# Scan-stage statistics moved from DVE to ACT and POOL, and expert gathers dealt out between the weight splits

## The chip, the cores and the metric

The kernel runs on one core of a Trainium2 chip. The time is the device time of one execution in microseconds (us). Three runs are shown: 2676.52, 2685.60 and 2686.33 us, median 2685.6. The profile is of one further execution. Engines: PE is TensorE (PEld its weight loads), DVE is VectorE, ACT is ScalarE, POOL is GpSimd, SP is SyncE, which issues most of the DMAs.

## The reference, cut to what matters

Two layers on x of shape (4, 512, 512): cross-attention and a gated feed-forward with Hadamard rotations, then a selective scan and a routed mixture of experts. Of it this case needs:

```
# layer norm, ahead of each block
(x - mean) / sqrt(var + 1e-5)
# layer 0 feed-forward: gate and up (512 -> 2048), silu(gate) * up, down (2048 -> 512), added to x
# layer 1 scan: 4 batches x 512 channels x 16 states, along 512 tokens
state = state * exp(delta * A) + (delta * u) * B_t ;  y_t = sum over states of state * C_t
y = (y + D * u) * silu(z)        # z: the layer norm of x; y is added to x
# layer 1 experts: 16 experts 512 -> 256 -> 512, two chosen for each of the 2048 tokens,
# silu(x Wg) * (x Wu) Wd, weighted and summed, beside one shared expert
```

## The kernel before, in words

`build` (L2700) runs stages one after the other, with a barrier of all engines behind each: `stage_norm`, `stage_attention`, `stage_prep`, `stage_mix`, `stage_norm_router`, `stage_experts`, `stage_combine`. Within a stage every engine has its own program, and the order is written out by hand; semaphores tie them together. The residual `xs` stays in SBUF, 16 tiles of 128 tokens x 512 (4 batches of TB = 4).

**The scan stage** (`stage_mix`, L1383) does two things at once: the feed-forward of layer 0 and the scan of layer 1. It has 64 steps s = 16 b + j: batch b, and j both a block of 128 hidden columns of the feed-forward and a scan state. In each step TensorE makes `gate` and `up` for two steps ahead (12 products each) and one `down` (four fp32 products) for three steps back. ACT makes four `decay` (an Exp into a PSUM tile) and one `silu`, and needs two table loads for it. POOL makes four `force` (the drive term, L1786) and three `add` (L1771), over a ring of RING = 4 tiles. DVE makes four `scan` (L1839, then a product L1850, for the first channel tile also a sum L1856), one `inner` (hT, L1864) and one `add_y` (L1870, adds the down product to x). The decays use two PSUM tiles in turn (BANKS = 2), so that decay q waits for the product of scan q - 2:

```
if ft == 0 and fn:
    act.wait_ge(s_add, dve_adds(fp, fn))
else:
    act.wait_ge(s_term, q - BANKS + 1)
```

In steps 0 to 3 of a batch DVE also makes `bn_stats` of one tile of the next batch (`normal_stats`, L1873) and one of the batch before, whose feed-forward is complete by then (`gate_stats`, L1877). At step 4 `spread` (L1879) turns them into `rstd` and `shift`: `bn_aggr`, then `newton_rsqrt` (L104), 14 operations of 4 or 8 columns that each wait for the one before, and the shift. From these, ACT normalizes the next batch (`norm`, L1687, from step 4) for its rotation, and makes `z` (L1713, steps 7 to 10) for the gating of the batch before. POOL has `skip_add` (four a batch at steps 1 to 3) and `gated` (steps 8 to 11). Behind the last step a tail does the last four downs, their statistics, `spread`, `z`, the gating and the transposes, one after the other.

**The expert stage** (`stage_experts`, L2424). The (token, choice) pairs lie sorted by expert in TILES = 47 tiles of 128 rows. For tile k: ACT copies the gathered rows (`fetch`, L2537), TensorE turns them, ACT and DVE split them into a high and a low part (fp32r), TensorE makes the gate and up product (`exp_g`, 12 products), ACT the SiLU, DVE the product, then the down product. The rows come by 47 indirect DMAs which POOL issues (L2507), all of them ahead of its other work, in groups; a group's rows are told to ACT (`s_rows`) when the next group is issued. Weights: SP loads each expert in three pieces into `raw` (two buffers) and `raw_down` (one); the next down piece waits until the one before is split. The split makes w = high + low in a ring of WRING = 3 experts. DVE makes the first three, high and low, ahead of its tiles (L2579, L2581); POOL the other 13 (L2522, L2525), each when the expert three before it is finished:

```
end = pool.value_load(plan.ends[0:1, e - WRING:e - WRING + 1], min_val=0, max_val=TILES)
wait_apart(pool, s_y, end + 2, s_pace)
```

## Time and profile before

| | |
|---|---|
| runs (median; lowest, highest) | 2685.6 us (2676.52; 2686.33) |
| the profiled execution | 2678.03 us |
| its span, first to last instruction | 2676.2 us |
| busy in the span: PE, DVE, ACT, POOL | 2285.0 (85%), 1848.7 (69%), 1229.4 (46%), 1354.8 us (51%) |
| mean granted TensorE clock | 0.926 |
| first and last scan start (L1839) | 1434.8 and 2140.5 us |
| first gather and first product of the experts | 2297.9 and 2328.4 us |
| last expert product starts | 2615.6 us |
| first gather of the combine stage | 2620.96 us |

Busy shares of the whole span mix stages with different limits; the rows below are of single stretches. In a timeline a bracket gives the idle time of the engine ahead of the instruction and what ended it. In a group, "x16 | 10.9, 682" is 16 instructions, 10.9 us in all, 682 ns each on average.

### The profile page before, as it was taken

To read this page: it belongs to the slowest core of one execution; us is meant where nothing else is said; L and a number is where in the kernel's file an instruction comes from. 1 tells how busy PE (TensorE), PEld (TensorE's weight loads), DVE (VectorE), ACT (ScalarE), POOL (GpSimd) and SP (SyncE) were. 2 spreads that over 40 slices of the span, in tenths; PEclk is the share of its full clock that TensorE was granted. 3 is DMA by queue.
4 is the path that set the end of the run, shared out by engine and by line. 5 is a ranking of instruction groups with operands and counts; after the bars stand their busy time and mean duration, and the time that the engine had idled before them with its cause. 6 is when DMAs were issued, how large, how long until landed. Compare 5 with 4: busy or idle time off the path is not lost. (4 is left out here: it accounts for less than half of the span.)

```text
span 2676.2 us, 35075 instructions
## 1 busy us (share of the span) xinstructions
PE 2285.0 (85%) x10784; PEld 1760.5 (66%) x10785; DVE 1848.7 (69%) x3381; ACT 1229.4 (46%) x2129; POOL 1354.8 (51%) x1088
## 2 busy tenths in 40 slices
PE   3799999999999999998774998897998969468980
PEld 2688888878888888887433665665665547347770
DVE  6577776767676777766775999999999976312223
ACT  2344444544454544444573655655655622124430
POOL 0233333333333333333584888878978931678324
PEclk7799999999999999999887999998998988789995
DMA  7512232222323122220557555564665321765317
GB/s 283 221 67 88 87 111 88 85 74 84 111 87 112 68 87 87 87 88 20 185 194 226 173 183 189 172 197 142 208 183 163 122 83 48 248 170 176 121 51 263
DMA packets 136761, 363.49 MB, mean 136 GB/s; under 512 B 21264, under 2 KB 58768, under 8 KB 118416
## 3 DMA queue, kind: packets, MB, share of 16 engines
q1 hardware_dynamic: 123504, 328.30, 35.8%
q0 software_dynamic: 6320, 20.71, 2.5%
q10 hardware_dynamic: 6768, 12.32, 1.2%
q8 instruction: 94, 1.54, 0.2%
q14 instruction: 75, 0.61, 0.1%
HBM read 289.99 MB, written 71.30 MB: 135 GB/s over the span
## 5 line engine op out<-in xcount | busy, mean ns | idle before, releaser
L641 POOL TENSOR_SCALAR att_probs<-att_probs,att_recip 128x512 f32<-128x512 f32 x256 | 182.1, 714 | 560.8 <-DVE att_recip L708 560.8
L1786 POOL TENSOR_TENSOR mix_drive<-mix_du,mix_rows 128x512 f32<-128x512 f32 x256 | 326.7, 1283 | 63.0 <-DMA mix_rows<-bc_d 24.5
L565 ACT ACTIVATE att_probs<-att_s,att_bias,att_rq 128x512 f32<-128x512 f32 x256 | 200.5, 783 | 287.6 <-DVE att_bias L704 287.2
L1839 DVE TENSOR_TENSOR_SCAN mix_state<-mix_state,mix_drive 128x512 f32<-128x512 f32 x256 | 312.7, 1221 | 16.1 <-POOL mix_drive L1786 11.6
L1670 ACT ACTIVATE mix_state<-mix_delta,mix_a 128x512 f32<-128x512 f32 x256 | 176.7, 691 | 278.4 <-DVE mix_drive L1850 238.6
L1771 POOL TENSOR_TENSOR mix_y<-mix_y,mix_drive 128x512 f32<-128x512 f32 x180 | 230.8, 1282 | 78.7 <-DVE mix_drive L1850 78.7
L1579 PE MATMUL mix_down<-mix_wd,mix_hT 128*128 128x512 f32 x512 | 232.7, 597 | 8.6 <-DVE residual_x L1870 8.6
L703 DVE TENSOR_REDUCE att_nmax<-att_s 128x1 f32<-128x512 f32 x256 | 174.9, 683 | 69.3 <-PE att_s L101 62.0
L744 DVE TENSOR_TENSOR att_pT<-att_pt,att_pT 128x512 fp32r<-128x512 f32 x256 | 170.0, 685 | 65.6 <-ACT att_pT L571 61.6
L571 ACT CAST att_pT<-att_pt 128x512 fp32r<-128x512 f32 x256 | 144.2, 593 | 133.0 <-PE att_pt L422 128.7
L99 PE MATMUL att_w<-att_w_qkv,att_cx 128*128 128x256 f32 x512 | 158.4, 309 | 34.5 <-DVE att_w_qkv L690 26.4
L1579 PEld LDWEIGHTS mix_down<-mix_wd,mix_hT 128*128 128x128 f32 x512 | 97.5, 191 | 110.5 <-issue 96.2
L101 PE MATMUL att_w<-att_w_qkv,att_cx 128*128 128x256 f32 x512 | 152.5, 298 | 0.0
L100 PE MATMUL att_w<-att_w_qkv,att_cx 128*128 128x256 f32 x512 | 152.3, 297 | 0.0
L422 PE MATMUL att_pt<-att_ident,att_probs 128*128 128x128 f32 x1024 | 142.1, 277 | 6.6 <-DVE att_pT L744 2.3
L650 POOL TENSOR_TENSOR att_rq<-att_qss,att_power 128x8 f32<-128x8 f32 x32 | 55.6, 1737 | 159.2 <-DVE att_qss L740 159.2
L422 PEld LDWEIGHTS att_pt<-att_ident,att_probs 128*128 128x128 f32 x1024 | 118.8, 144 | 22.1 <-DVE att_pT L744 12.0
L99 PEld LDWEIGHTS att_w<-att_w_qkv,att_cx 128*128 128x128 f32 x512 | 105.0, 205 | 39.8 <-issue 37.3
L1850 DVE TENSOR_TENSOR mix_drive<-mix_state,mix_rows 128x512 f32<-128x512 f32 x180 | 124.4, 691 | 6.2
L99 PE MATMUL exp_g<-exp_w,exp_xT 128*128 x188 | 81.9, 436 | 53.2 <-POOL exp_w L2525 34.8
L579 ACT CAST att_oT<-att_o 128x512 fp32r<-128x512 f32 x64 | 37.7, 589 | 181.0 <-PE att_o L101 181.0
L99 PE MATMUL att_s<-att_kT,att_qT 128*128 128x512 f32 x256 | 106.7, 417 | 14.0 <-issue 9.1
(356 smaller groups left out, 6655.5 us busy)
## 6 DMA issues: line engine op xcount, KB each, us to landing
att_xn<-normT SPq DMA_DIRECT2D x32, 2048.0 KB, 8.7
mix_gu<-guT SPq DMA_DIRECT2D x64, 1024.0 KB, 8.2
mix_rows<-bc_d SPq DMA_DIRECT2D x128, 256.0 KB, 5.1
guT<-att_ffnT SPq DMA_DIRECT2D x32, 512.0 KB, 5.7
mix_wd<-wdT SPq DMA_DIRECT2D x16, 1024.0 KB, 7.8
slots<-exp_y ACTq DMA_DIRECT2D x47, 256.0 KB, 2.0
normT<-nrm_outT SPq DMA_DIRECT2D x4, 2048.0 KB, 9.1
exp_raw<-in_L_ffn_Wg SPq DMA_DIRECT2D x16, 512.0 KB, 5.8
```

Source lines behind the costliest of these rows:

```text
L99: pe.matmul(out, lh, rh, start=start, stop=False)
L101: return pe.matmul(out, ll, rh, start=False, stop=stop)
L422: tr = pe.transpose(ps_pt[(b + n) % 2][:, t, :], probs[:, h * TB + t, k * P:(k + 1) * P], ident_sb[:, :])
L565: act.activation(probs[:, n, :], ps_s[n % 2][:, :], ACT.Exp, bias=bias[:, n:n + 1], scale=rq[:, n:n + 1], accum_out=sums[:, n:n + 1]).then ...
L641: pool.tensor_scalar(probs[:, n, :], probs[:, n, :], recip[:, n:n + 1], 1.0, ALU.mult, ALU.mult).then_inc(s_pn, 1)
L703: own.after(dve.tensor_reduce(nmax[:, n:n + 1], ps_s[n % 2][:, :], AX_X, ALU.max, negate=True))
L744: dve.tensor_tensor(pT[:, 1, k, :], ps_pt[(b + (TB + 1) * h + k) % 2][:, :, :].rearrange("p t n -> p (t n)"), pT[:, 0, k, :].bitcast(F32), ...
L1579: mm = pe.matmul(ps_y[:, :], hT[c % 2][:, k, tok], wd[c % 2][:, k, :], start=(k == 0), stop=(k == CHUNK - 1))
L1670: act.activation(state[q % BANKS][:, :], delta[i % DELTAS][:, :], ACT.Exp, scale=a[:, t, n:n + 1]).then_inc(s_decay, 1)
L1771: pool.tensor_tensor(out[:, :], out[:, :], drive[q % RING][:, :], ALU.add).then_inc(s_padd, 1)
L1786: pool.tensor_tensor(drive[q % RING][:, :], du[i % DUS][:, :], rows[g % ROWS][:, 0, :], ALU.mult).then_inc(s_drive, 1)
L1839: dve.tensor_tensor_scan(h[:, :], h[:, :], drive[q % RING][:, :], 0.0, ALU.mult, ALU.add).then_inc(s_scan, 1)
```

## The change

In the scan stage the statistics leave DVE. ACT makes them in steps 0 to 3 (`stats`), behind the step's last decay: for each tile an Identity whose accumulator gives the sum, a multiply that gives the negative mean, and a Square of x minus the mean whose accumulator gives the sum of squares; the full-size outputs go to `normT` and are not used. POOL makes `rstd` with `pow` and the shift (`spread`), at step 5, behind the first `add` and `force`. In the tail ACT and POOL do the same for the last batch. In the expert stage the gathers come in groups of 2, 6, 10, 16, 4, 4, 4 and 1: POOL issues the second group when expert 0's weights have landed, the third when expert 1's have, and the last four groups behind its splits of experts 3, 4, 5 and 6. ACT makes the high parts of the first three experts, DVE only the low ones, and the third expert's come behind tile 0. What is computed stays the same. The diff, cut:

```diff
+                summed, centred, squared = Steps(act, s_sums), Steps(act, s_minus), Steps(act, s_squares)
+
+                def moments(tiles):
+                    squared.wait()
+                    for c, row in tiles:
+                        summed.mark(act.activation(normT[:, c // TB, :], xs[:, row, :], ACT.Identity,
+                                                   accum_out=sums[:, c:c + 1]))
+                    summed.wait()
+                    for c, row in tiles:
+                        centred.mark(act.mul(minus[:, c:c + 1], sums[:, c:c + 1], -1.0 / DIM))
+                    centred.wait()
+                    for c, row in tiles:
+                        squared.mark(act.activation(normT[:, c // TB, :], xs[:, row, :], ACT.Square, bias=minus[:, c:c + 1],
+                                                    accum_out=squares[:, c:c + 1]))
+
+                def stats(b, t):
+                    tiles = []
+                    if b + 1 < B:
+                        tiles.append((t, (b + 1) * TB + t))
+                    if b:
+                        act.wait_ge(s_yadd, BLOCKS * (b - 1) + (CHUNK - 1) * TB + t + 1)
+                        tiles.append((TB + t, (b - 1) * TB + t))
+                        if t == 0:
+                            act.wait_ge(s_rot, KD * min(b, B - 1))
+                    moments(tiles)
...
@@ -1736,6 +1763,10 @@
                     if s + 1 < ALL:
                         decay(q + 2)
                         decay(q + 3)
+                    if j < TB:
+                        stats(b, j)
+                    if j == TB:
+                        squared.wait()
...
                 for t in range(TB):
+                    stats(B, t)
+                for t in range(TB):
...
+                def spread(b, done):
+                    c = slice(0 if b + 1 < B else TB, 2 * TB if b else TB)
+                    if b and b + 1 < B:
+                        pool.wait_ge(s_nrm, TB * b)
+                    if b >= 2:
+                        pool.wait_ge(s_z, TB * (b - 1))
+                    pool.wait_ge(s_squares, done)
+                    pool.tensor_scalar(var_eps[:, c], squares[:, c], 1.0 / DIM, LN_EPS, ALU.mult, ALU.add).then_inc(s_var, 1)
+                    pool.wait_ge(s_var, b + 1)
+                    pool.tensor_tensor(rstd[:, c], var_eps[:, c], power[:, c], ALU.pow).then_inc(s_root, 1)
+                    pool.wait_ge(s_root, b + 1)
+                    pool.tensor_tensor(shift[:, c], minus[:, c], rstd[:, c], ALU.mult).then_inc(s_rs, 1)
...
                     for q in range(ET * (s + 1), ET * (s + 2)):
                         add(q - RING)
                         if s + 1 < ALL:
                             force(q)
+                        if j == TB + 1 and q % ET == 0:
+                            spread(b, moments_made(b))
...
                     skip_add(B - 1, t)
+                spread(B, moments_made(B))
...
-                def normal_stats(b, t):
-                    own.mark(dve.bn_stats(stats[:, t, :], xs[:, b * TB + t, :]))
-
-                def gate_stats(b, t):
-                    dve.wait_ge(s_yadd, BLOCKS * b + (CHUNK - 1) * TB + t + 1)
-                    own.mark(dve.bn_stats(stats[:, TB + t, :], xs[:, b * TB + t, :]))
-
-                def spread(first, last):
-                    c = slice(first, last)
-                    own.wait()
-                    for t in range(first, last):
-                        own.mark(dve.bn_aggr(meanvar[:, t, :], stats[:, t, :]))
-                    own.wait()
-                    own.after(dve.tensor_scalar(var_eps[:, c], meanvar[:, c, 1], LN_EPS, None, ALU.add))
-                    newton_rsqrt(dve, own, rstd[:, c], var_eps[:, c], guess[:, c], newton[:, c])
-                    dve.scalar_tensor_tensor(shift[:, c], meanvar[:, c, 0], -1.0, rstd[:, c], ALU.mult,
-                                             ALU.mult).then_inc(s_rs, 1)
...
-                    if j < TB:
-                        if b + 1 < B:
-                            normal_stats(b + 1, j)
-                        if b:
-                            gate_stats(b - 1, j)
-                    if j == TB:
-                        if b and b + 1 < B:
-                            dve.wait_ge(s_nrm, TB * b)
-                        if b >= 2:
-                            dve.wait_ge(s_z, TB * (b - 1))
-                        spread(0 if b + 1 < B else TB, 2 * TB if b else TB)
...
                 for n in range(ALL - LAG - 1, ALL):
                     add_y(n)
-                    gate_stats(B - 1, n % TB)
-                dve.wait_ge(s_z, TB * (B - 1))
-                spread(TB, 2 * TB)
...
-    GROUPS = [4, 4] + [8] * 4 + [7]
+    GROUPS = [2, 6, 10, 16, 4, 4, 4, 1]
...
+                def gather(g):
+                    for k in range(sum(GROUPS[:g]), sum(GROUPS[:g + 1])):
                         pool.indirect_dma_start(rows[:, k, :], None, xn,
                                                 bass.IndirectOffsetOnAxis(plan.source[:, k:k + 1], 0)
                                                 ).then_inc(s_gather[g], 16)
-                        k += 1
-                    if g:
-                        pool.wait_ge(s_gather[g - 1], 16 * GROUPS[g - 1])
-                        pool.sem_inc(s_rows, GROUPS[g - 1])
-                pool.wait_ge(s_gather[-1], 16 * GROUPS[-1])
-                pool.sem_inc(s_rows, GROUPS[-1])
-                for e in range(WRING, EXPERTS):
+
+                def gathered(g):
+                    pool.wait_ge(s_gather[g], 16 * GROUPS[g])
+                    pool.sem_inc(s_rows, GROUPS[g])
+
+                def loaded(e):
+                    for _, _, sem, value in pieces(e):
+                        pool.wait_ge(sem, value)
+
...
+                gather(0)
+                loaded(0)
+                gather(1)
+                gathered(0)
+                loaded(1)
+                gather(2)
+                gathered(1)
+                gather(3)
+                gathered(2)
+                for e in range(WRING, EXPERTS):
+                    g = e - WRING + 3
+                    split(e)
+                    if g < len(GROUPS):
+                        gathered(g)
+                    if g + 1 < len(GROUPS):
+                        gather(g + 1)
...
+                def split_hi(e):
+                    for src, cols, sem, value in pieces(e):
+                        act.wait_ge(sem, value)
+                        act.copy(w[:, e, 0, cols], src[:, :]).then_inc(s_split, 1)
-                tiles(act, step)
+                fetch(0, 0)
+                fetch(1, 1)
+                split_hi(0)
+                x_hi(0, 0)
+                split_hi(1)
+                tiles(act, step, lambda: split_hi(2))
...
-                for e in range(WRING):
+                def split_lo(e):
                     for n, (src, cols, sem, value) in enumerate(pieces(e)):
                         dve.wait_ge(sem, value)
-                        dve.tensor_copy(w[:, e, 0, cols], src[:, :]).then_inc(s_split, 1)
                         dve.wait_ge(s_split, 2 * e + n + 1)
                         dve.tensor_tensor(w[:, e, 1, cols], src[:, :], w[:, e, 0, cols].bitcast(F32),
                                           ALU.subtract).then_inc(s_w if n else s_wpart, 1)
...
-                tiles(dve, step)
+                split_lo(0)
+                x_lo(0, 0)
+                split_lo(1)
+                tiles(dve, step, lambda: split_lo(2))
```

## Rows read from the trace of the kernel before

**Rows 1.** Scan stage, second batch: us; PE, PEld, DVE, ACT, POOL busy; clock; DMA share; GB/s.

```profile
1608.00:1790.00 182.00, 166.22 (x580) 108.91 (x580) 166.56 (x215) 105.97 (x129) 154.82 (x123) 0.96 0.56 179
```

**Rows 2.** Groups of instructions, DVE: line, operation, count, busy us, mean ns, idle before.

```profile
L1877 DVE BATCH_NORM_STATS2 mix_stats<-residual_x 128x6 f32<-128x512 f32 x16 | 10.9, 682 | 0.1
```

**Rows 3.** Tile mix_hT (made once a step), windows: count, min/median/max ns, first and last start.

```profile
L1864 DVE SCALAR_TENSOR_TENSOR mix_hT<-mix_up,mix_up_scale,mix_sil x5: 749/750/751, 1449.6 to 1488.7; 128x512 f32<-128x512 f32 x5
...
L1864 DVE SCALAR_TENSOR_TENSOR mix_hT<-mix_up,mix_up_scale,mix_sil x2: 751/751/751, 1488.7 to 1504.4; 128x512 f32<-128x512 f32 x2
...
L1864 DVE SCALAR_TENSOR_TENSOR mix_hT<-mix_up,mix_up_scale,mix_sil x5: 741/749/751, 1618.4 to 1665.7; 128x512 f32<-128x512 f32 x5
...
L1864 DVE SCALAR_TENSOR_TENSOR mix_hT<-mix_up,mix_up_scale,mix_sil x2: 741/746/752, 1665.7 to 1683.8; 128x512 f32<-128x512 f32 x2
...
L1864 DVE SCALAR_TENSOR_TENSOR mix_hT<-mix_up,mix_up_scale,mix_sil x5: 741/743/751, 1982.2 to 2027.2; 128x512 f32<-128x512 f32 x5
...
L1864 DVE SCALAR_TENSOR_TENSOR mix_hT<-mix_up,mix_up_scale,mix_sil x2: 743/746/749, 2027.2 to 2045.2; 128x512 f32<-128x512 f32 x2
```

**Rows 4.** Timeline of a plain step: start us, us, engine, line, operation.

```profile
1501.74 1.23 DVE L1839 TENSOR_TENSOR_SCAN mix_state<-mix_state,mix_drive 128x512 f32<-128x512 f32 x1 [0.29 <-ACT mix_state L1670]
...
1507.68 0.69 ACT L1670 ACTIVATE mix_state<-mix_delta,mix_a 128x512 f32<-128x512 f32 x1 [1.35 <-DVE mix_drive L1850]
...
1511.40 1.23 DVE L1839 TENSOR_TENSOR_SCAN mix_state<-mix_state,mix_drive 128x512 f32<-128x512 f32 x1
```

**Rows 5.** Groups of instructions, ACT.

```profile
L565 ACT ACTIVATE att_probs<-att_s,att_bias,att_rq 128x512 f32<-128x512 f32 x256 | 200.5, 783 | 287.6 <-DVE att_bias L704 287.2
...
L1670 ACT ACT_TABLE_LOAD x64 | 82.1, 1283 | 1.2
...
L565 ACT ACTIVATION_READ_ACCUMULATOR att_probs<-att_s,att_bias,att_rq 128x1 f32 x256 | 50.7, 198 | 0.0
...
L553 ACT ACTIVATE att_qsq<-att_w 128x512 f32<-128x512 f32 x64 | 40.9, 639 | 0.0
...
L1719 ACT ACTIVATE mix_a<-mix_a 128x64 f32<-128x64 f32 x1 | 0.3, 256 | 0.0
```

**Rows 6.** Waits in the scan loop: us in total, times, longest.

```profile
DVE mix_state L1839 <- POOL mix_drive L1786: 11.6, 7, 3.0
```

**Rows 7.** Groups of instructions, POOL.

```profile
L1786 POOL TENSOR_TENSOR mix_drive<-mix_du,mix_rows 128x512 f32<-128x512 f32 x256 | 326.7, 1283 | 63.0 <-DMA mix_rows<-bc_d 24.5 <-DVE mix_state L1839 15.4 <-DMA mix_du<-du_d 8.7
...
L650 POOL TENSOR_TENSOR att_rq<-att_qss,att_power 128x8 f32<-128x8 f32 x32 | 55.6, 1737 | 159.2 <-DVE att_qss L740 159.2
```

**Rows 8.** Timeline of the scan stage's tail: DVE, then ACT.

```profile
2161.04 0.69 DVE L1877 BATCH_NORM_STATS2 mix_stats<-residual_x 128x6 f32<-128x512 f32 x1
...
2165.44 3.16 ACT L1713 ACTIVATE mix_work<-residual_x,mix_shift,mix_rstd 128x512 f32<-128x512 f32 x4 [11.28 <-DVE mix_shift L1887]
```

**Rows 9.** Timeline of POOL in the expert stage.

```profile
2304.98 2.73 POOL L2507 DMA_INDIRECT exp_rows<-xrows,plan_source  x1 [0.30 <-issue]
...
2373.17 1.90 POOL L2522 TENSOR_SCALAR exp_w<-exp_raw 128x2048 fp32r<-128x2048 f32 x1 [8.60 <-issue]
```

**Rows 10.** Timeline of PE in the expert stage, idle time before in brackets.

```profile
2328.36 0.79 PE L99 MATMUL exp_g<-exp_w,exp_xT 128*128 x1 [15.69 <-DVE exp_w L2581]
...
2383.48 0.79 PE L99 MATMUL exp_g<-exp_w,exp_xT 128*128 x1 [21.82 <-POOL exp_w L2525]
...
2453.88 0.79 PE L99 MATMUL exp_g<-exp_w,exp_xT 128*128 x1 [5.05 <-POOL exp_w L2525]
```

**Rows 11.** A window, the opening of the expert stage; columns as in rows 1.

```profile
2297.00:2329.00 32.00, 2.71 (x10) 1.98 (x11) 17.48 (x14) 2.83 (x5) 25.60 (x19) 0.50 0.93 320
```

**Rows 12.** Timeline of DVE, group of ACT, landing of the down piece's loads.

```profile
2303.33 1.23 DVE L2579 CAST exp_w<-exp_raw 128x2048 fp32r<-128x2048 f32 x1 [11.52 <-DMA exp_raw<-in_L_ffn_Wu]
...
L2208 ACT CAST rou_w<-rou_raw 128x1024 fp32r<-128x1024 f32 x3 | 2.9, 1047 | 0.0
...
DMA to landing us min/median/max: 3.4/4.2/7.8
```

More of the change, by code:

```diff
@@ L1413, in stage_mix @@
         d = m.sb("skip", [P, ET])
-        stats = m.sb("stats", [P, 2 * TB, 6])
-        meanvar = m.sb("meanvar", [P, 2 * TB, 2])
+        sums = m.sb("sums", [P, 2 * TB])
+        minus = m.sb("minus_mean", [P, 2 * TB])
+        squares = m.sb("squares", [P, 2 * TB])
         var_eps = m.sb("var_eps", [P, 2 * TB])
-        guess = m.sb("guess", [P, 2 * TB])
-        newton = m.sb("newton", [P, 2 * TB])
+        power = m.sb("power", [P, 2 * TB])
         rstd = m.sb("rstd", [P, 2 * TB])
@@ L1809, in _ @@
                 pool.wait_ge(s_const, 64)
+                pool.wait_ge(s_power, 1)
                 for s in range(ALL):
@@ L1827, in _ @@
                     skip_add(B - 1, t)
+                spread(B, moments_made(B))
             @block.vector
             def _(dve):
-                own = Steps(dve, s_dve)
                 def scan(q):
@@ L2470, in part, with tiles @@
             return w[:, par, hl, at:at + n]
-        def tiles(eng, step):
+        def tiles(eng, step, third=None):
             step(0, 0)
+            if third:
+                third()
             pairs = (TILES - 3) // 2
@@ L2503, in _ @@
             def _(pool):
-                k = 0
-                for g, size in enumerate(GROUPS):
-                    for _ in range(size):
+                def gather(g):
+                    for k in range(sum(GROUPS[:g]), sum(GROUPS[:g + 1])):
                         pool.indirect_dma_start(rows[:, k, :], None, xn,
```

11 lines of the change are left out of this document (6 added, 5 removed).

## The prediction

> **What bounds the kernel now.** I read the stage windows first, then the groups by engine, then the timeline of the two stages that the diff touches, and the waits. Nothing outside the scan stage and the expert stage changes, so only these two are worked.
>
> *Scan stage, four batches of 16 steps.* In the window of the second batch VectorE (DVE) and TensorE are both busy 92% of 182 us, POOL 85%, ACT 58% [rows 1]. A step of the first batch takes 39.1 / 4 = 9.8 us [rows 3], and the plain step of the timeline is DVE work back to back: from the first scan to that of the next step 9.66 us, with no wait in it that is worth naming [rows 4]. So DVE sets the pace, TensorE is 8% behind. On that path stand 12 of the 16 gate statistics (4 are in the tail) and as many of the next batch, 0.68 us each [rows 2], and once a batch the small operations of `spread`: step 4 takes 15.7, 18.1 and 18.0 us where a plain step takes 9.8 [rows 3], thus 5.9 us in batch 0 and 8.2 us in the later ones. POOL is the bound in one place: DVE waited 11.6 us for its drive terms [rows 6], after the `skip_add`s of steps 1 to 3.
>
> *Expert stage.* TensorE starts its first product at 2328.36, released by DVE's split of expert weights, stands 21.8 us before tile 6 for expert 3's weights, which POOL splits only from 2373.17 on, behind all 47 gathers, and waits again for POOL at 2453.88 [rows 9, 10]. One split on POOL takes 10 us (2373.17 to TensorE's release at 2383.48). The opening 32 us have the DMA engines busy 93% at 320 GB/s [rows 11].
>
> **Part 1: what leaves DVE.** 24 x 0.70 = 17 us of `bn_stats` and 5.9 + 3 x 8.2 = 30.5 us of `spread`: 47 us if nothing took its place. The tail comes below.
>
> **Part 2: what ACT takes.** One tile needs an Identity with accumulator, a read of it, a tiny multiply, a Square with bias and accumulator, and a read. Nearest rows: 0.64 us for a Square without pointers, 0.78 for an Exp with two pointers and an accumulator, 0.20 for the read, 0.26 for a 64-wide multiply [rows 5]. I take 0.70, 0.20, 0.20, 0.75, 0.20 and 0.1 for each of three waits on its own semaphores, an estimate: 2.35 us for one tile, 4.4 us for two. Bounds: 0.64 an operation and free waits give 3.8 us for two tiles, 0.78 an operation and 0.2 a wait, with 0.26 for the multiply, 5.0 us.
> This block stands before the next `decay` on ACT, and DVE's next scan waits for that. In the plain step the last decay starts 5.94 us after the first scan and ends at 6.63 [rows 4]; with a block M and the next decay (0.69) the next step's first scan can start at 7.3 + M. For two tiles (batches 1 and 2) 11.7 us; for one tile 9.65, just under the 9.8 us that DVE needs. So in batches 1 and 2 the four steps take 46.8 us where they take 47.3 now: the DVE time that is freed turns into a wait for ACT, and POOL's lag, now covered by it, I cost at 0.5 us. In batch 0 no down product is added yet, DVE needs 9.1 us: 39.1 becomes 36.7, a gain of 2.4. In batch 3 POOL is the bound: DVE work is 9.8 + 0.7 a step, 42 us, and 45.0 are taken [rows 3]; POOL's work stays, so with less on DVE its wait grows by as much: gain 0.
>
> **Part 3: `spread` on POOL.** One multiply-add, one `pow` (1.74 us for 8 columns [rows 7], about 1.0 for 4, an estimate at half the columns and some fixed cost) and one product; the two others have no row of that size, I take 0.3 each with waits (from nothing to 1.0). 2.4 us for 8 columns, 1.7 for 4. It stands behind POOL's first `add` and `force` (1.28 us each [rows 7]) of the next step. `norm` on ACT waits for it at step 4, in front of the next decay. Counted from the end of the step's first term: POOL done at 2.56 + 2.4 = 5.0 without lag; two `norm` 1.6, decay 0.7: 7.3, against 7.0 at which DVE wants it. In batch 0 that is nearly nothing: 15.7 becomes 9.9, gain 5.8. In batches 1 and 2 POOL still lags by about 2.3 us (an estimate: DVE's waits of up to 3.0 us for it [rows 6] show that its ring of four is used up), so DVE stands 2.5 us: 18.1 becomes 12.3, gain 5.8 each. In batch 3 there is no `norm`, the ring is used up, `spread` adds 1.7 less the 0.8 that POOL gains a step: 18.0 becomes 10.7, gain 7.3.
> Scan loop: 2.4 + 5.8 + 5.8 + 5.8 + 7.3 = 27.1 us.
>
> **Part 4: the tail.** Now 4.4 us pass from the last `bn_stats` to the first `z` [rows 8]. After: 2.35 on ACT and 1.7 + 0.2 on POOL. I cost it at nothing; ACT stood idle 11.3 us there, which hides the other three tiles and the table load.
>
> **Part 5: experts.** Removed: the three hi copies of DVE, which go to ACT (1.05 us for 1024 columns [rows 12], so 3.1 us an expert); the first product no longer waits for experts 1 and 2. But `fetch` of tiles 0 and 1 now stands ahead of `split_hi(0)`, and the row counter rises only after the next group's gathers: two gathers (2.5 us), weights of expert 0 landed (2303.33 for the two large pieces [rows 12], the down piece about 2305), six gathers of 1.25: rows known at 2312.8. Fetches 1.2, hi 3.0, lo of the last piece 1.2: expert 0 ready at about 2319, its first product 2320, 8 us earlier. Yet `fetch(2)` waits for ten more gathers, and these for the down piece of expert 1, whose load waits for expert 0's split: 2319 plus 4.2 to 7.8 us of landing [rows 12], less now that no gathers run beside it: 2324.5. Tile 2's row is known at 2338, so the SiLU of tile 0 comes some 3 us later than now. That is hidden by tile 6: what counts is POOL's chain. From 2324.5: 26 gathers 32.5, stretching 2.6, seven splits of 10.06, 13 gathers between them 16.3: the split that releases the product of 2453.88 now [rows 10] ends at 2446.3, not 2453.5. The stalls at the end are bound to tiles and keep their length. Gain 7.4 us (0.2 less at an extra 1.3 us at tile 17, inside it). Bounds: gathers stretched throughout as the worst ones of the opening (2.73 us where 0.95 is usual [rows 9]) would eat all of it and 15 more; landing at once gives 12.
> The stretched gathers ran beside DVE's splits [rows 9, 12]. *The Trainium skill, SBUF — State Buffer, "Who interferes with whom", has a copy or cast of DVE in its two-port mode lock GpSimd out of writing descriptors, and a tensor_tensor with two SBUF inputs contend with reads only. The row disagrees in part: the 2.73 us gather began with the subtraction, after the copy. By the page the copies' move to ACT would end the stretching and give 10 us here; by the row it stays beside the three subtractions, the 2.6 us above.*
>
> **Sum.** The profiled execution took 2678.0 us (span 2676.2 and 1.8 around it). 2678.0 - 27.1 - 7.4 = 2643.5. The runs shown lie from 1.5 below to 8.3 above it, the median 7.6 above; I add about half, 4.5: 2648 us, 1.4% under the median.
>
> **Rivals.** (A, the forecast, 0.54.)
> B, 0.17: ACT's block hides better than I count (decays and block interleave, POOL catches up in the wait), and most of the 47 us is kept. For: ACT is busy only 58%. Against: the ring of two state banks, which forces its order. Batches 1 and 2 would give up to 6 more each, batch 3 another 3: 2633.
> C, 0.18: POOL's chain in the expert stage gains nothing, since the load of expert 1's down piece comes late and gathers now stand in front of each split; or M is 5.0. Against: 21.8 us of wait are there to be taken. 2648 + 7 = 2655, with the larger block 2661.
> D, 0.06, the slower side: each block needs another table. Place: the first Square, and the next Exp behind it. Price: two loads of 1.28 us (64 of them stand before the Exps now [rows 5]) for 16 blocks is 41 us, all on the path since one-tile steps have 0.15 us to spare: 2648 + 41 = 2689. It decides once any function of the block is not in Exp's set. The rows speak against it: attention runs its Squares among its Exps and the groups of ACT have no table load on those lines. *The Trainium skill, ScalarE: Activation LUTs, "Table sets", names only the cheap functions such as copy and identity as part of every set, and Square is not in that list; by it 2689.*
> E, 0.05: the part taken from DVE only makes TensorE the bound (92% now), with gains of 15 in all: 2670.
>
> **Numbers.** 0.5%, 13.4 us, is what a measurement here can tell from no change: faster means under 2672. A, B and nearly all of C lie there, E half: 0.83 with room for what I did not see taken off, 0.82. Slower (over 2699) needs D and more: 0.05. Same 0.13. The range is from just under B, 2632, to 2670, which takes in C with its larger block and the bounds of M.
>
> **What would show it.** Right: no `bn_stats` in the scan stage; steps 0 to 3 of batches 1 and 2 at 11.7 us with DVE idle 2 us a step, released by ACT's decay; step 4 at 12 us; no new table load; first expert product at 2320 less the shift, the wait before tile 6 down from 21.8 to a few us, a new one of 8 to 20 before tile 7; the product after split 9 some 7 us earlier relative to the stage's start. Wrong: table loads in the block, a block over 5.0 us, POOL waiting on ACT's squares at step 5, gathers of 1.5 us and more throughout.

## The result, and the profile after

The kernel after takes 2645.7 us (median of 4 runs, 2642.79 to 2650.47), the kernel before, measured beside it, 2681.1 (2674.77 to 2686.33): a ratio of 0.987, interval 0.9847 to 0.9894. The forecast was 2648 us. The profiled execution took 2645.5 us (span 2643.4).

The stages are cut at the first load that each issues. The expert stage after, for one, goes from 2270.6 to 2587.9, which is 317.3 us:

```profile
L2512 SPq DMA_DIRECT2D exp_ident<-in_ident x1: 345/345/345, 2270.6 to 2270.6; - x1
...
L2719 SPq DMA_DIRECT2D com_acc<-mixed x4: 367/501/625, 2587.9 to 2589.4; - x4
```

| us | scan stage begins | scan stage | router | experts | combine |
|---|---|---|---|---|---|
| before | 1411.3 | 763.8 | 122.0 | 323.1 | 55.9 |
| after | 1415.5 | 733.0 | 122.1 | 317.3 | 55.5 |

The scan stage gained 30.8 us and the experts 5.8. The stages ahead of them, whose code is the same, took 4.2 us more in this execution; over the kernels below the scan stage begins anywhere from 1411 to 1426 us. So I read stages, and totals only beside them.

**Scan stage.** The rows that answer to [rows 3], for batches 0, 1 and 3 (step 1's hT to step 5's, then to step 6's):

```profile
L1916 DVE SCALAR_TENSOR_TENSOR mix_hT<-mix_up,mix_up_scale,mix_sil x5: 750/751/752, 1454.4 to 1491.1; 128x512 f32<-128x512 f32 x5
...
L1916 DVE SCALAR_TENSOR_TENSOR mix_hT<-mix_up,mix_up_scale,mix_sil x2: 750/750/751, 1491.1 to 1500.8; 128x512 f32<-128x512 f32 x2
...
L1916 DVE SCALAR_TENSOR_TENSOR mix_hT<-mix_up,mix_up_scale,mix_sil x5: 741/743/751, 1614.5 to 1659.4; 128x512 f32<-128x512 f32 x5
...
L1916 DVE SCALAR_TENSOR_TENSOR mix_hT<-mix_up,mix_up_scale,mix_sil x2: 742/746/750, 1659.4 to 1672.8; 128x512 f32<-128x512 f32 x2
...
L1916 DVE SCALAR_TENSOR_TENSOR mix_hT<-mix_up,mix_up_scale,mix_sil x5: 741/743/752, 1963.3 to 2008.1; 128x512 f32<-128x512 f32 x5
...
L1916 DVE SCALAR_TENSOR_TENSOR mix_hT<-mix_up,mix_up_scale,mix_sil x2: 741/746/751, 2008.1 to 2018.0; 128x512 f32<-128x512 f32 x2
```

| us | batch 0 | batch 1 | batch 3 |
|---|---|---|---|
| four steps with statistics, before / forecast / after | 39.1 / 36.7 / 36.7 | 47.3 / 47.3 / 44.9 | 45.0 / 45.0 / 44.8 |
| the step with `spread`, before / forecast / after | 15.7 / 9.9 / 9.8 | 18.1 / 12.3 / 13.5 | 18.0 / 10.7 / 9.9 |

(For batch 1 the forecast 46.8 of the block plus the 0.5 that I gave to POOL's lag.) By batches of 16 steps the gains are 8.7, 7.5, 7.4 and 7.0 us, together 30.6 against a forecast of 27.1.

The block on ACT in batch 1, two tiles (start us, duration us, as in a timeline):

```profile
1617.76 0.69 ACT L1671 ACTIVATE mix_state<-mix_delta,mix_a 128x512 f32<-128x512 f32 x1 [1.35 <-DVE mix_drive L1902]
1618.38 0.61 ACT L1722 ACTIVATE mix_normT<-residual_x 128x512 f32<-128x512 f32 x1
1618.90 0.19 ACT L1722 ACTIVATION_READ_ACCUMULATOR mix_normT<-residual_x 128x1 f32 x1
1619.00 0.61 ACT L1722 ACTIVATE mix_normT<-residual_x 128x512 f32<-128x512 f32 x1
...
1619.74 0.29 ACT L1726 ACTIVATE mix_minus_mean<-mix_sums 128x1 f32<-128x1 f32 x2
1620.06 0.72 ACT L1729 ACTIVATE mix_normT<-residual_x,mix_minus_mean 128x512 f32<-128x512 f32 x1
...
1621.49 1.28 ACT L1671 ACTIVATE mix_state<-mix_delta,mix_a 128x512 f32<-128x512 f32 x2
```

From 1618.38 to the next decay at 1621.49 are 3.1 us, not 4.4. The starts of two operations of 0.61 us lie 0.62 apart with a read of the accumulator of 0.19 between them. The two decays behind the block take 1.28 us together, at 0.69 each, so neighbours without a read overlap by 0.1 us; the read costs this overlap and no more. A wait on the block's own semaphore costs about 0.03 us. There is no table load. *The Trainium skill, ScalarE: Activation LUTs, "What ACT_TABLE_LOAD costs", gives an ACTIVATE 186 ns plus 0.833 ns a column, 93 ns more for a pointer, and an overlap of 93 ns between neighbours: for 512 columns 0.61 and 0.71 us. The rows agree, with 0.61 and 0.72. Its "Table sets" doesn't list Square among the functions of every set; here Square ran between Exps without a load.*

So the floor of a step with two tiles is 7.3 + 3.1 = 10.4 us; the first two of batch 1 take 10.4 and 10.6, the other two 12.0 and 11.9. What stands there is in the waits of DVE and ACT in the scan loop (us in total, times, longest):

```profile
DVE mix_state L1891 <- POOL mix_drive L1819: 17.3, 10, 2.2
DVE mix_state L1891 <- ACT mix_state L1671: 12.9, 6, 3.7
```

```profile
ACT mix_work L1688 <- POOL mix_shift L1851: 9.9, 3, 4.7
```

DVE's wait for POOL's drive terms was 11.6 us [rows 6] and is 17.3: DVE now gets to it sooner. Its wait for ACT's decays, the second line, was 4.5 before. The stretch of batch 1, in the columns of [rows 1], has TensorE busy 95% (165.0 of 174 us), DVE and POOL 89% each:

```profile
1612.00:1786.00 174.00, 164.98 (x579) 107.40 (x577) 154.16 (x183) 117.18 (x168) 155.35 (x125) 0.98 0.57 187
```

`spread` on POOL, and ACT behind it:

```profile
1665.72 0.20 POOL L1847 TENSOR_SCALAR mix_var_eps<-mix_squares 128x8 f32<-128x8 f32 x1
1666.01 1.67 POOL L1849 TENSOR_TENSOR mix_rstd<-mix_var_eps,mix_power 128x8 f32<-128x8 f32 x1
1667.75 0.20 POOL L1851 TENSOR_TENSOR mix_shift<-mix_minus_mean,mix_rstd 128x8 f32<-128x8 f32 x1
...
1668.04 1.52 ACT L1688 ACTIVATE mix_work<-residual_x,mix_shift,mix_rstd 128x512 f32<-128x512 f32 x2 [4.73 <-POOL mix_shift L1851]
```

It takes 2.2 us (forecast 2.4) and ACT waits 4.7 us for it, since POOL comes to it late.

In the tail the last statistics of [rows 8] are replaced by this; from the end of the last `add_y` at 2135.16 to `z` are 3.6 us where 4.4 were, and a table load is hidden in it:

```profile
2134.47 0.69 DVE L1922 TENSOR_TENSOR residual_x<-mix_down,residual_x 128x512 f32<-128x512 f32 x1 [3.79 <-PE mix_down L1580]
...
2137.02 1.28 ACT L1714 ACT_TABLE_LOAD   x1
...
2138.80 3.16 ACT L1714 ACTIVATE mix_work<-residual_x,mix_shift,mix_rstd 128x512 f32<-128x512 f32 x4 [0.49 <-POOL mix_shift L1851]
```

**Expert stage.** Timelines of POOL, ACT and PE; they answer to [rows 9, 10, 12]:

```profile
2271.40 1.23 POOL L2529 DMA_INDIRECT exp_rows<-xrows,plan_source  x1 [13.22 <-POOLq L75]
...
2280.34 0.94 POOL L2529 DMA_INDIRECT exp_rows<-xrows,plan_source  x1 [6.46 <-DMA exp_raw_down<-in_L_ffn_Wd]
...
2282.55 1.14 ACT L2579 COPY exp_row<-exp_rows 128x512 f32<-128x512 f32 x2 [26.21 <-POOLq L2535]
...
2289.89 0.79 PE L99 MATMUL exp_g<-exp_w,exp_xT 128*128 x1 [4.54 <-DVE exp_w L2628]
...
2293.80 0.95 POOL L2529 DMA_INDIRECT exp_rows<-xrows,plan_source  x1 [5.09 <-DMA exp_raw_down<-in_L_ffn_Wd]
...
2297.82 0.62 ACT L2579 COPY exp_row<-exp_rows 128x512 f32<-128x512 f32 x1 [3.21 <-POOLq L2535]
...
2327.51 1.93 POOL L2547 TENSOR_SCALAR exp_w<-exp_raw 128x2048 fp32r<-128x2048 f32 x1
...
2337.91 0.79 PE L99 MATMUL exp_g<-exp_w,exp_xT 128*128 x1 [6.71 <-POOL exp_w L2550]
...
2352.78 0.79 PE L99 MATMUL exp_g<-exp_w,exp_xT 128*128 x1 [8.07 <-POOL exp_w L2550]
```

The first product comes 18.5 us behind the first gather (30.4 before). The 21.8 us before tile 6 are 6.7, and a new wait of 8.1 stands before tile 7. The rows of tiles 0 and 1 are known at 2282.55, 11.1 us behind the first gather, while four of the six gathers of the next group are still to start: POOL's sequencer raises the counter ahead of the gathers that stand queued before it, and doesn't wait for them to be written. So tile 2's row comes at +26.4 us.

POOL begins the first split (expert 3) 56.9 us into the stage, before at 76.0. A part of this is in [rows 9]: of the 8.60 us in front of the split before, 7.4 are the wait until the last gathers have landed; their semaphore's last update is recorded at 2371.98, and reading the table of tile counts takes the rest. After, that split waits for no gather of the group ahead of it, and begins right behind the last one; against this stand the two waits for weights, 6.5 and 5.1 us, in the lines above.

ACT's waits in the tiles:

```profile
ACT exp_hid L2603 <- PE exp_g L101: 69.7, 38, 11.2
...
ACT exp_y L2607 <- DMA slots<-exp_y: 27.2, 10, 5.5
```

The second line is new in size: the one output buffer `yout` is not free until its store has landed, 27.2 us in ten waits against 20.9 before, when the longest was 3.0.

### The profile page after: what moved, and what is told of

Same layout as the page of the kernel before. It is cut to its first block and busy times, and to the rows that moved or that the text cites. A ratio compares the mean times of both kernels' runs of the same rounds, so it can differ in the third digit from the quotient of the medians.

```text
span 2643.4 us, 35123 instructions
## 1 busy us (share of the span) xinstructions
PE 2284.0 (86%) x10784; PEld 1760.5 (67%) x10785; DVE 1797.4 (68%) x3239; ACT 1279.1 (48%) x2275; POOL 1356.7 (51%) x1104
## 5 line engine op out<-in xcount | busy, mean ns | idle before, releaser
L1891 DVE TENSOR_TENSOR_SCAN mix_state<-mix_state,mix_drive 128x512 f32<-128x512 f32 x256 | 312.9, 1222 | 30.8 <-POOL mix_drive L1819 17.3
L749 DVE TENSOR_TENSOR att_oT<-att_o,att_oT 128x512 fp32r<-128x512 f32 x64 | 44.2, 691 | 106.7 <-ACT att_oT L579 106.7
```

The source lines that it names most:

```text
L1891: dve.tensor_tensor_scan(h[:, :], h[:, :], drive[q % RING][:, :], 0.0, ALU.mult, ALU.add).then_inc(s_scan, 1)
```

## The experiments

Each ratio is against runs of the kernel before that were measured beside it. Kernels e1 and e2 take the stages apart: e1 has the scan stage of after and the expert stage of before, e2 the other way round.

> The new scan stage with the expert stage of before. The scan stage (from the first load of the log decays to the first load of the router) took 763.8 us before and 733.0 after, the expert stage (first load to the first load of the combine stage) 323.1 and 317.3. If the two parts add up, this kernel is 31 us faster than before (2681 - 31 = 2650) and the expert stage stays at 323. Rival: part of the scan stage's gain is an upstream or clock effect of the joint kernel; then the gain here is under 26 us.

> The scan stage of before with the new expert stage. If the parts add up: 6 us faster than before (2675), with the first expert product about 9 us earlier in its stage and the wait before tile 6 replaced by two waits of about 7 and 8 us. Rival, as I forecast blind: 7.4 us. Rival: no gain at all, since the chain of weight splits on POOL only moves its waits; then 0 within 2 us.

e1: 2652.7 us (2646.52 to 2655.75), ratio 0.988 (0.9857 to 0.9904); scan stage 733.2, experts 324.3. e2: 2676.1 us, ratio 0.9973 (0.996 to 0.9987); scan stage 765.2, experts 317.2. The parts don't touch each other: 1.2% and 0.27% add up to 1.5%, inside the interval of the whole (1.1% to 1.5%), and each stage has the length that it has in after or, where its code is the old one, in before, within 1.5 us.

**e3, `spread` back on DVE**, the moments still on ACT:

```diff
+                    dve.wait_ge(s_squares, done)
+                    own.after(dve.tensor_scalar(var_eps[:, c], squares[:, c], 1.0 / DIM, LN_EPS, ALU.mult, ALU.add))
+                    newton_rsqrt(dve, own, rstd[:, c], var_eps[:, c], guess[:, c], newton[:, c])
+                    dve.tensor_tensor(shift[:, c], minus[:, c], rstd[:, c], ALU.mult).then_inc(s_rs, 1)
...
+                    if j == TB:
+                        spread(b, moments_made(b))
```

> The changed kernel with the step from the sums to 1/std and shift put back on DVE (Newton steps, at step 4), the statistics still on ACT. Theory: most of the gain is the small serial operations leaving DVE. Before they took 5.9 us in batch 0 and 8.2 in the others; coming back they cost 5.9 in batch 0, about 4.6 in batches 1 and 2 (step 4 goes from 13.5 to 18.1 us), 6 to 8 in batch 3 and 2 in the tail: 23 us slower than the changed kernel (2669), so that the statistics alone are worth 8 us. Rival: the statistics are worth their full 24 x 0.7 = 17 us and the small operations the rest: 14 us slower (2660).

2668.1 us (2664.16 to 2672.32), ratio 0.9948 (0.9928 to 0.9968). The scan stage takes 757.2 us, 24.2 more than after. Batch 1 of e3, as above:

```profile
L1913 DVE SCALAR_TENSOR_TENSOR mix_hT<-mix_up,mix_up_scale,mix_sil x5: 743/743/750, 1618.7 to 1663.6; 128x512 f32<-128x512 f32 x5
...
L1913 DVE SCALAR_TENSOR_TENSOR mix_hT<-mix_up,mix_up_scale,mix_sil x2: 743/747/751, 1663.6 to 1681.6; 128x512 f32<-128x512 f32 x2
```

The four steps keep their 44.9, the next takes 18.0 as before. So of the 30.8 us of the scan stage the moments on ACT give about 6.6 and `spread` on POOL 24.2.

**e4, the block made twice:**

```diff
                     moments(tiles)
+                    moments(tiles)
```

> The changed kernel with ACT's block of statistics made twice in each step (the same values). The block took 3.1 us for two tiles and 1.65 for one. Theory: a step of batches 1 and 2 cannot be shorter than 7.3 us plus the block, as the next decay stands behind it; with 6.2 us the four steps take 13.5 us each, 54 where 44.9 are taken now, in batch 0 they take 10.0 instead of 9.2, batch 3 about 1 more in all, the tail 1.7: 24 us slower than the changed kernel (2670). Rival: ACT is busy only two thirds of the time there and the block hides in its idle time: 2 to 4 us slower, from the tail alone.

2663.8 us (2657.22 to 2676.26), ratio 0.9928 (0.9907 to 0.9949); 18.1 us slower than after where I expected 24; scan stage 752.6, 19.6 more. Batch 1 of e4:

```profile
L1917 DVE SCALAR_TENSOR_TENSOR mix_hT<-mix_up,mix_up_scale,mix_sil x5: 744/751/752, 1629.8 to 1684.2; 128x512 f32<-128x512 f32 x5
...
L1917 DVE SCALAR_TENSOR_TENSOR mix_hT<-mix_up,mix_up_scale,mix_sil x2: 750/750/751, 1684.2 to 1694.7; 128x512 f32<-128x512 f32 x2
```

54.4 / 4 = 13.6 us a step, which is 7.3 + 2 x 3.1 and 0.1: the floor holds. And step 4 falls from 13.5 to 10.4: while the others waited for ACT, POOL caught up. So 9.5 us more in the four steps cost 6.4 in the batch. In after POOL's lag carries the two slow steps and what is over 10.4 in step 4.

**e7 and e8 test whether POOL is that bound.** e7 takes away the product D * u that POOL makes in `skip_add` (1.57 us, 16 times), so its output lacks D. e8 makes the product on ACT instead, behind the SiLU of steps 1 and 3, with POOL's two later additions both in step 3. It changes one thing more: the last of the four loads of `u` is issued at step 2 and no longer at step 3.

```diff
                     if b >= 1 and j == 2:
                         load_u(b - 1, 2)
-                    if b >= 1 and j == 3:
                         load_u(b - 1, 3)
...
+                def skip_part(b, t):
+                    n = ET * b + t
+                    act.wait_ge(s_u[t % 2], 16 * (n // 2 + 1))
+                    act.activation(work[t % 2][:, :], work[t % 2][:, :], ACT.Identity, scale=d[:, t:t + 1]).then_inc(s_skip, 1)
...
+                    if b >= 1 and j in (1, 3):
+                        skip_part(b - 1, j - 1)
+                        skip_part(b - 1, j)
...
-                    pool.tensor_scalar(work[t % 2][:, :], work[t % 2][:, :], d[:, t:t + 1], None, ALU.mult).then_inc(s_skip, 1)
```

> The changed kernel without the product D * u on POOL (u is added without D, so this leaves out that factor). Theory: in steps 1 to 4 of batches 1 to 3 POOL is the bound (12.0, 11.9 and 13.5 us where ACT's block allows 10.4). With 6.3 us less on POOL in each batch, batches 1 and 2 become 4 to 5 us shorter and batch 3 5 us: 14 us faster than the changed kernel (2632). Rival: ACT's block is the bound in these steps and POOL only waits less: 0 to 3 us.

> The changed kernel with the product D * u made by ACT, two at step 1 and two at step 3 behind the SiLU, where ACT has 1.2 us to spare; POOL only adds. If POOL is the bound there and ACT's gap is free, most of what the run without the product gains comes back as a real gain: 10 to 12 us faster than the changed kernel (2635). Rival: ACT is as full as POOL, the second product of a step pushes a decay back, and only half is gained: 5 us.

e7: 2644.3 us (2643.55 to 2644.98), ratio 0.9846 (0.9829 to 0.9863); scan stage 726.8, 6.2 less than after. I had expected 14 us; the whole gained only 1.4, since the expert stage, whose code is the same, took 320.1 us in it (the stall told at the end). Part of the 25 us that POOL was freed of came back as waits of POOL for `u`, whose next load waits for its own addition, and DVE still waits for POOL's drive terms (17.3 us in after); step 4 of batch 1 still takes 13.4:

```profile
POOL mix_y L1830 <- DMA mix_work<-u_d: 8.2, 4, 2.9
...
DVE mix_state L1889 <- POOL mix_drive L1819: 8.4, 5, 3.4
```

e8: 2630.3 us (2628.6 to 2631.15), ratio 0.9795 (0.9778 to 0.9812); scan stage 713.2, 19.8 less than after, nearly twice what I expected. Batches 1 and 3 of e8:

```profile
L1924 DVE SCALAR_TENSOR_TENSOR mix_hT<-mix_up,mix_up_scale,mix_sil x5: 744/751/751, 1612.2 to 1653.6; 128x512 f32<-128x512 f32 x5
...
L1924 DVE SCALAR_TENSOR_TENSOR mix_hT<-mix_up,mix_up_scale,mix_sil x2: 751/752/752, 1653.6 to 1664.0; 128x512 f32<-128x512 f32 x2
...
L1924 DVE SCALAR_TENSOR_TENSOR mix_hT<-mix_up,mix_up_scale,mix_sil x5: 751/751/752, 1948.0 to 1987.2; 128x512 f32<-128x512 f32 x5
...
L1924 DVE SCALAR_TENSOR_TENSOR mix_hT<-mix_up,mix_up_scale,mix_sil x2: 751/751/751, 1987.2 to 1996.9; 128x512 f32<-128x512 f32 x2
```

All four steps of batch 1 run at the floor of 10.4, the step with `spread` too (10.4 instead of 13.5), and batch 3 at 9.8. DVE's wait for POOL is gone from its list, and POOL no longer waits for `u`. This shows POOL's lateness as the cause of what steps 1 to 5 of a batch have above the floor in after. It doesn't show the product alone as the cause: taking away only the product (e7) gave 6.2 of these 19.8 us, and how the rest divides between the earlier load of `u` and the place of the additions was not run.

**e5, all gathers ahead of the splits**, in after's order otherwise:

```diff
+                for g in range(4, len(GROUPS)):
+                    gather(g)
+                    gathered(g - 1)
+                gathered(len(GROUPS) - 1)
                 for e in range(WRING, EXPERTS):
-                    g = e - WRING + 3
                     split(e)
-                    if g < len(GROUPS):
-                        gathered(g)
-                    if g + 1 < len(GROUPS):
-                        gather(g + 1)
```

> The changed kernel with the last 13 gathers issued ahead of the split of expert 3, as before the change, and not between the splits; the new opening (gathers held back for the weights, high parts on ACT) stays. Theory: the wait before tile 6 moves: the split of expert 3 starts 16 us later (73 us into the stage, not 57), the SiLU of tile 6 comes at 88 us (72 with the change, 92 before it), then the splits run without gathers and the tiles without the gathers' traffic, so that tile 18 comes at 161 us (157 with the change, 161 before): 4 us slower than the changed kernel. Rival: the new opening alone makes the stage's gain and the mixing is worth nothing; then this is the same within 1 us.

2659.4 us (2655.02 to 2661.6), ratio 0.9905 (0.9887 to 0.9922); expert stage 330.5, 13.2 more than after and 7.4 more than before. Split 3 begins 80.1 us into the stage; after has 56.9. Thirteen gathers are 16.3 us of that. The other 6.9 are a wait of POOL to which the profile gives no releaser:

```profile
2346.28 1.90 POOL L2547 TENSOR_SCALAR exp_w<-exp_raw 128x2048 fp32r<-128x2048 f32 x1 [6.83 <-issue]
```

It is the wait of [rows 9] again: the split stands behind the landing of the last gathers, whose last semaphore update is recorded at 2345.04. So split 3 begins 4.1 us later in its stage than before: with all gathers in front, POOL's waits for weights cost more than the new opening gives. My 4 us for the loss were far too few, and the rival (no loss) is out. How large it is stays less sure than 13.2: e5 shows the stall told at the end, and e7 and e8, which have the expert stage of after and the stall too, take 320.1 and 322.0, so that 8.5 to 10.4 us are left. What gains is the mixing of gathers and splits; the earlier first expert alone gains nothing.

**e6, a second buffer and semaphore for the stores of the tiles** (`rows[:, 0, :]`, free behind its fetch):

```diff
-        yout = m.sb("y", [P, DIM])
+        yout = [m.sb("y", [P, DIM])[:, :], rows[:, 0, :]]
...
-                        wait_apart(act, s_st, 16 * k, s_pace)
-                        act.copy(yout[:, :], ps_y[1 - i][:, :]).then_inc(s_yout, 1)
+                        wait_apart(act, s_st[1 - i], k * 8 + 8 * i, s_pace)
+                        act.copy(yout[1 - i], ps_y[1 - i][:, :]).then_inc(s_yout, 1)
```

> The changed kernel with two store buffers for the experts' output instead of one (the second is the place of tile 0's rows, which are used up). With the gathers in among the tiles ACT waited 27 us for stores, where it waited 21 before, and tiles 11 to 13 took 21 us instead of 16. Theory: these waits are what lost 2 of the 7.4 us that I forecast, and more; without them the split of expert 8 starts at 125 us of the stage and not 131, and the stage is 5 to 6 us shorter (312 instead of 317). Rival: the DMA engines are simply full there, and the wait goes on to the rows or weights: at most 1 us.

2635.1 us (2633.46 to 2638.65), ratio 0.9816 (0.9798 to 0.9834). Expert stage 309.0, 8.3 less than after; the waits for stores are gone and split 8 begins at 127.1 us of the stage instead of 130.7. So the store buffer was the loss that my sum of Part 5 didn't have. (e6 has the stall as well; beside e7 and e8 the second buffer gives 11 to 13 us.)

**e9, e8 and e6 together.**

> The skip product on ACT and the two store buffers together. If the two act in different stages and do not touch, the mixer stage keeps the 713.2 us that it had with the skip product alone and the expert stage takes the 309.0 us that it had with two store buffers alone: 2645.7 - 19.8 - 8.3 = about 2618 us. Rival: with the skip product alone the expert stage came out at 322.0 us instead of 317.3, with a stall of some 20 us between the products of tile 2 and their evaluation that the kernel after does not have; if that stall comes with the longer instruction stream of the mixer stage, the expert stage keeps 4 to 5 us of it and the time is about 2622 us.

2615.4 us (2607.11 to 2618.48), ratio 0.9737 (0.9714 to 0.976); scan stage 713.6, experts 306.0. The gains add up.

**e10 and e11, smaller gather groups ahead of the first split**, 16 gathers instead of 34, in e10 on after and in e11 on e9:

```diff
-    GROUPS = [2, 6, 10, 16, 4, 4, 4, 1]
+    GROUPS = [2, 6, 4, 4, 6, 6, 8, 8, 3]
```

> The kernel after with gather groups of 2, 6, 4, 4, 6, 6, 8, 8 and 3 instead of 2, 6, 10, 16, 4, 4, 4 and 1: before the first split on POOL (expert 3) stand 16 gathers instead of 34, so 18 gathers x 1.25 = 22 us less. Theory (the splits of experts 3 and 4 set the opening, and they come late because of the gathers ahead of them): split 3 starts at about 43 us of the stage instead of 56.9, bound by expert 0's tiles, split 4 at about 61 instead of 71.8; the waits of TensorE before tiles 6 and 7 (13 and 16 us between evaluations) shrink to one of about 5, and since later splits follow with 7.5 us of gathers between them, the store waits and the splits of 5 to 8 give part back: the expert stage 303 to 310 us instead of 317.3, the time 2632 to 2639 us. Rival (the store waits or POOL's whole load of 47 gathers and 13 splits set the stage whatever the order): the waits only move to tiles 10 to 20, the stage stays within 3 us of 317.3 and the time within 3 us of 2645.7.

> The skip product on ACT, the two store buffers and the small groups together. Theory (three independent limits: POOL in the scan loop, the store of the tiles, the gathers ahead of the splits): mixer stage 713 us, expert stage 290 to 300 us, since with no store wait the tiles run at 4.9 us and the early splits are in time: 2645.7 - 19.8 - 17 to -27 = 2599 to 2609 us. Rival (POOL's load sets the expert stage): expert stage at about 309 as with the two store buffers alone, 2618 us.

e10: 2637.9 us (2635.93 to 2638.34), ratio 0.9824 (0.9808 to 0.984), expert stage 310.3: the time is inside the theory's range, the stage at its upper edge (7.0 us less than after). e11: 2619.9 us (2615.04 to 2622.43), ratio 0.9755 (0.9738 to 0.9771), expert stage 312.4 where e9 has 306.0: both of my cases missed. Split 3 begins at 41.5 us of the stage, yet split 8 at 130.5 where e9 has 123.8. The 6.7 us are in one row of e11:

```profile
2293.37 1.92 POOL L2555 TENSOR_SCALAR exp_w<-exp_raw 128x2048 fp32r<-128x2048 f32 x1 [6.58 <-PE exp_y_ps L101]
```

POOL stood still, since expert 0's tiles weren't done, with gathers left to issue. From there to split 8 POOL has no pause in either kernel, and the same gathers and splits to do. In after POOL does pause: it ends split 7 at 123.6 us of the stage and begins split 8 at 130.7, so there was something to gain by order, and e10 gained it. That is e12's theory: once POOL works without a pause, not the order but its load up to split 9 counts.

**e12, e9 with gathers moved behind split 9** (32 ahead of it instead of 47; the 34 in the expectation is two too many):

```diff
-    GROUPS = [2, 6, 10, 16, 4, 4, 4, 1]
+    GROUPS = [2, 6, 6, 6, 2, 2, 2, 2, 2, 2, 2, 3, 5, 5]
```

> The kernel with the skip product on ACT and two store buffers (2615.4 us), with its 47 gathers spread: groups of 2, 6, 6, 6 ahead of the split of expert 3, 2 behind each of the next seven splits, then 3, 5 and 5, so 34 gathers instead of 47 stand before the split of expert 9. Theory, from the small groups' failure beside two store buffers (expert stage 312.4 instead of 306.0 us): POOL works without a pause from the opening to the split of expert 9, so its load up to there (gathers x 1.25 us + 7 splits x 10.1 us + 14 us of waits for weights) sets the stage, and the order within it does not matter. 13 gathers fewer are 16 us: split 9 ends at about 129 us of the stage instead of 144, tile 18 is evaluated at about 134 instead of 149, the stage takes about 291 us and the kernel about 2600 us. Rival: the tiles themselves (4.7 to 5.3 us each on ACT and TensorE) or the loads of weights become the limit at once, and the stage falls by less than 6 us, to 300 us or more, the time 2610 us or more.

2599.5 us (2598.51 to 2601.15), ratio 0.9686 (0.9661 to 0.9711), the fastest of all. Expert stage 293.3 (expected 291); split 9 ends at 127.7 us of it (129), tile 18 is evaluated at 133.0 (134). POOL's end of split 9, two gathers, split 10:

```profile
2377.97 1.04 POOL L2537 DMA_INDIRECT exp_rows<-xrows,plan_source  x1 [0.15 <-issue]
2379.32 0.95 POOL L2537 DMA_INDIRECT exp_rows<-xrows,plan_source  x1 [0.30 <-issue]
2380.29 1.92 POOL L2555 TENSOR_SCALAR exp_w<-exp_raw 128x2048 fp32r<-128x2048 f32 x1
```

Both groupings (e10's and e12's) are fitted to this data: a split waits for tiles of an earlier expert, and their rows must have been told by then. If the first expert had so many tiles that some of their gathers stood behind that split, POOL and the tiles would wait for each other for ever.

## Why the prediction was right

The forecast of 2648 us stands against 2645.7. The steps, one by one:

- **Part 2, the term that was mis-sized.** "2.35 us for one tile, 4.4 us for two" (bounds 3.8 to 5.0) measured 1.7 and 3.1: below the lower bound, since that had the reads of the accumulator and the operations one behind the other. By the real block the floor is 10.4, not 11.7. In the first two steps of batches 1 and 2 the path was as forecast, with only this term too large.
- **"POOL's lag, now covered by it, I cost at 0.5 us"** held only with the long block. With the short one POOL becomes the bound from the third step on (12.0 and 11.9 us). Measured 44.9 where 47.3 was forecast; without the lag it would be 41.5 (e8). The two errors had opposite signs.
- **Batch 0** (8.2 forecast for its two terms, 8.3 measured) held as a number. Its working doesn't hold together: by the prediction's own floor of 9.65 the four steps would take 38.6 and not 36.7. e4, where batch 0 takes 10.2 us a step with a block of about 3.4, puts the floor there at 6.8 plus the block, and so under DVE's 9.2. **Batch 3** (four steps 45.0, measured 44.8, bound by POOL as said) held.
- **Part 3.** `spread` took 2.2 us where 2.4 was forecast. In batches 1 and 2 step 4 came out at 13.5 instead of 12.3: my estimate of 2.3 us for POOL's lag was too low, for the same reason; e4, where POOL had caught up, has 10.4. e3 prices the part at 24.2 us; my four terms had 24.7.
- **Part 4**, costed at nothing, gained 0.8.
- **Part 5.** "Tile 2's row is known at 2338", 40 us behind the first gather, is the step that failed: it was 26.4. I had the row counter rise only when the next group's gathers were written. The SiLU of tile 0 came 9 us earlier than before, not 3 later. The failure cost nothing, as this was hidden. POOL's chain started 4 to 6 us sooner than forecast (third group at +22.4 us where I had +26.6, first split at +56.1 against +61.7), with the new wait before tile 7 at 8.1, the foot of "8 to 20"; but by split 9 that lead was spent and more: it ended 4.9 us earlier than before instead of 7.2 (the prediction's own two times differ by 7.2; its 7.4 is not explained). The stretching of gathers, put at 2.6 us for the last 26, was 1.5 there and 1.2 in the six before (2.12, 2.15 and 1.22 us where 0.95 is usual), each time beside a subtraction on DVE, with every copy on ACT: the row's reading held. The tiles between took 5.9 to 8.7 us for the store buffer, and split 8 waited for them. e6 shows that loss.
- **The sum.** Scan loop 30.6 for 27.1, experts 5.8 for 7.4, stages ahead +4.2 for 0, allowance to the median +0.2 for 4.5: errors of 3.5, 1.6, 4.2 and 4.3, which mostly cancelled. That the total came so close is partly luck.
- **Rivals.** B (the block hides better) had its mechanism come true by half: the block was short, but POOL took most of what that gave. C was wrong in the experts and D has no table load. E isn't the case yet: in e8 the steps shrank further with the same products on TensorE. There it is busy 154.4 of 160 us, so little more can be had before it is the bound.

## What to carry to other kernels

When work leaves the bounding engine, what counts is the next resource on the ring, here POOL; look for the smallest thing that it can hand over, and for what it waits for once it has (16 products of 1.57 us taken away gave 6 us of a stage; moved to ACT, with the load behind them issued earlier, 20). Where an engine works without a pause up to a point that releases others, reordering within gives nothing (e11; e10 gained because POOL still had a pause), and moving work past that point gives its full length (e12). A store with one buffer is a wait that shows only when the stage gets faster.

## What was not expected of the hardware

**A stall of TensorE's results while gathers run.** In e8 the last product of tile 2 starts at 2287.00 by its record, and ACT evaluates it 21 us later, though nothing else that it waits for is late. The profile names transfers of earlier stages, which means that it found no releaser:

```profile
2287.00 0.39 PE L101 MATMUL exp_g<-exp_w,exp_xT 128*128 x1
```

```profile
2308.31 0.38 ACT L2611 ACTIVATE exp_hid<-exp_g 128x256 f32<-128x256 f32 x1 [17.26 <-DMA mix_du<-du_d]
```

```profile
2308.62 1.90 POOL L2555 TENSOR_SCALAR exp_w<-exp_raw 128x2048 fp32r<-128x2048 f32 x1 [3.81 <-DMA rou_raw<-in_L_ffn_sWd]
```

The update of the semaphore behind that product is recorded at 2308.29, so the signal was late and not ACT. It ends 3.5 us after POOL's last gather of the group. The same is in e5, e6, e7 and e9 (gaps of 14 to 27 us between evaluations at tiles 2 and 3), and in none of the other nine kernels. It makes split 3 begin at 60.5 instead of 56.9 us in e6 and e8, and the expert stage of e8 322.0 long instead of 317.3.

What starts it stays open. The stage's own code alone does not: e7 and e8 have after's, and after, e2, e3 and e4 have it without the stall. Two rivals stand. The chip may matter: e1 to e4 ran on one chip and e5 to e11 on another, where all five with after's groups stall (they have 16 gathers in a row or more) and e10 and e11, with small groups, don't. And recording may play a part: of the 256 semaphore updates that the group of 16 gathers makes, 28 to 38 are recorded in the five stalled traces and all 256 in those of after and e2 to e4; but e10 to e12 lack records too, without a stall. No run tells these apart.

**Squares between Exps need no table load**, and 8-column `pow` on POOL takes 1.67 us, eight times a product of that size (0.20), yet is far cheaper than the 14 small dependent operations on DVE. In batch 1 before, these took 6.7 us, because four of them lasted 1.1 to 1.2 us each where the others took 0.17; in the tail before, where none did, 2.8 us. What lengthened the four was not looked into.

**POOL's semaphore increments run ahead of its gathers**, as told above: a counter raised behind a queue of gathers rose while four of them had still to start.
